# Last slot of a 16-batch transformer kernel: the last batch's gated result in two token halves, routing sums moved to ScalarE, and products that nobody reads in a pause of TensorE

## The reference, cut to what matters

```
# L1 attention, per head of 64 values
o = chunk_retention(rotary(q), rotary(k), v)
o = o * rsqrt(mean(o*o) + EPS) * gnorm_w
o = o * (g * sigmoid(g))
x = x + o @ Wo.T
# L1 feed-forward: half of the tokens of a batch are routed
h = layernorm(x); scores = h @ w_router
top_scores, top_idx = top_k(scores, 256)
update = sigmoid(top_scores) * (gelu(h[top] @ W1 + b1) @ W2 + b2)
x = x + 0.5 * (h with the update added at top_idx)
```

## Time and profile before

| | us |
|---|---|
| median of 3 runs | 805.19 |
| the profiled execution | 807.99 |
| its span, first to last instruction | 805.8 |
| TensorE busy | 757.8 (94%) |
| VectorE busy | 665.8 (83%) |
| ScalarE busy | 424.5 (53%) |
| GpSimd busy | 475.3 (59%) |
| mean granted clock of TensorE | 0.977 |

### The profile page before, as it was taken

The page is one execution under the profiler, slowest core; times in us unless marked ns, Lnnn a source line. Parts: engine busy times, 40 slices in busy tenths (PEclk is TensorE's granted clock), DMA queues, the critical chain, the costliest instruction groups (busy, mean ns, idle before and its releaser), DMA issues.

```text
span 805.8 us, 29577 instructions
## 1 busy us (share of the span) xinstructions
PE 757.8 (94%) x13001; PEld 614.8 (76%) x13001; DVE 665.8 (83%) x1825; ACT 424.5 (53%) x875; POOL 475.3 (59%) x375
## 2 busy tenths in 40 slices
PE   5778999999999999998999999999999999999875
PEld 4666888787887787776878888877888888878653
DVE  6686888888888999997858889987777988888887
ACT  2333555565555565654554446655544565564745
POOL 4467888887888888876543444444434344453544
PEclk9996999999999999999999999999999999999988
DMA  7000100011111110010000000000000000000113
GB/s 229 30 28 29 29 28 16 16 28 29 29 28 30 28 29 2 3 55 3 1 2 2 3 3 2 2 2 2 3 2 2 3 2 2 3 2 16 55 39 105
DMA packets 23284, 18.57 MB, mean 23 GB/s; under 512 B 2146, under 2 KB 20468, under 8 KB 22900
## 3 DMA queue, kind: packets, MB, share of 16 engines
q1 hardware_dynamic: 22596, 16.40, 7.0%
q10 hardware_dynamic: 560, 0.28, 0.1%
HBM read 12.48 MB, written 4.19 MB: 21 GB/s over the span
## 4 chain that ended last, share of the span: by engine, by line
PE 75%; DVE 17%; POOL 3%; ACT 2%; issue 1%; DMA 0%; DVEq 0%; POOLq 0%; ACTq 0%
PE ps L286 20%; PE ps L410 11%; PE ps L401 10%; PE ps L281 5%; PE ps L675 4%; PE ps L364 3%; PE ps L308 3%; PE ps L297 3%; PE ps L384 3%; PE ps L394 2%; POOL grstd L1067 2%; PE ps L356 2%; DVE x L1225 2%; PE ps L667 2%; PE ps L320 2%; PE ps L685 2%
## 5 line engine op out<-in xcount | busy, mean ns | idle before, releaser
L1067 POOL TENSOR_TENSOR grstd<-gve,mhalf 128x32 f32<-128x32 f32 (+1 forms) x32 | 159.0, 4968 | 26.5 <-DVE gve L1280 26.5
L410 PEld LDWEIGHTS ps<-w_s,hid 128*128 128x128 f32 x1024 | 123.5, 192 | 9.0 <-issue 8.0
L410 PE MATMUL ps<-w_s,hid 128*128 128x128 f32 x1024 | 129.0, 277 | 0.7 <-issue 0.7
L401 PE MATMUL ps<-xt_r,w_s 128*128 128x512 f32 x256 | 126.7, 617 | 0.7 <-ACT xt_r L822 0.7
L826 ACT ACTIVATE hid<-ps,b_s 128x512 f32<-128x512 f32 x128 | 84.0, 726 | 24.0 <-PE ps L401 23.8
L1063 POOL TENSOR_TENSOR r_ret<-ve_ret,powers 128x8 f32<-128x8 f32 x32 | 57.8, 1807 | 27.6 <-DVE ve_ret L1211 27.6
L286 PE MATMUL ps<-w_qkvg,xt_p 128*128 128x128 f32 x512 | 71.2, 285 | 2.8 <-ACT xt_p L822 2.8
L1073 POOL TENSOR_TENSOR um<-um 128x96 f32<-128x96 f32 (+1 forms) x32 | 21.3, 665 | 88.5 <-DVE um L1259 88.5
L401 PEld LDWEIGHTS ps<-xt_r,w_s 128*128 128x128 f32 x256 | 45.2, 192 | 35.1 <-issue 30.1
L1058 POOL TENSOR_TENSOR rstd_ln_mod<-ve_ln_mod,mhalf 128x4 f32<-128x4 f32 x32 | 32.3, 1010 | 65.3 <-DVE ve_ln_mod L1211 65.3
L1253 DVE TENSOR_TENSOR sc<-ps,tri 128x1024 f32<-128x1024 f32 (+1 forms) x64 | 58.3, 953 | 15.1 <-PE ps L320 7.6
(11 more groups left out here) (236 smaller groups left out, 1749.8 us busy)
## 6 DMA issues: line engine op xcount, KB each, us to landing
xtin<-in_xt SPq DMA_DIRECT2D x16, 256.0 KB, 3.8
out_x<-base SPq DMA_DIRECT2D x16, 256.0 KB, 2.3
xin<-in_x SPq DMA_DIRECT2D x15, 256.0 KB, 3.0
rot<-in_rot SPq DMA_DIRECT2D x2, 1024.0 KB, 5.9
w_s<-in_w SPq DMA_DIRECT2D x2, 256.0 KB
xin<-in_x ACTq DMA_DIRECT2D x1, 256.0 KB, 4.0
w_qkvg<-in_wqkvg SPq DMA_DIRECT2D x1, 256.0 KB, 3.8
w_qkv<-in_wqkv SPq DMA_DIRECT2D x1, 256.0 KB
```

Source lines behind the costliest of these rows:

```text
L401: nc.tensor.matmul(bank(k), w1_s[:, f, :], xt["r"][:].rearrange("p j n -> p (j n)"), start=True, stop=True).then_inc(s[f"h{f}"], 1)
L410: mm = nc.tensor.matmul(bank(k, j * P, P), hid[:, f, j * P:(j + 1) * P], w2_s[:, f, :], start=False, stop=(f == last and j == NT - 1), ski ...
L1067: nc.gpsimd.tensor_tensor(grstd[:, 0:n], gve[:, 0:n], mhalf[:, 0:n], ALU.pow) \
```

## The change

In the last slot:

1. Batch 15's y is transposed with a signal after each half (two token tiles). Squares, sums over heads, the powers and the final multiplication go by halves. y is multiplied by the gate first (signal yg), by the norm's factor second (gy_half). The transposes of the gated result, their copies and the output products go by halves as well.
2. TensorE issues 18 products of the identity with itself into bank 6 behind the transposes of y (keep_busy(18, X1)), and 5 such products in the first slot. Nobody reads them.
3. The base of batches 14 and 15 is computed by ScalarE, four instructions each (scaled_base), from x2 with a scale 1 + 0.5 rstd and a bias of half the negative mean; VectorE makes these two small columns (base_weights) instead of keep_base. Batch 15 uses the buffer x2b.
4. The order on TensorE and VectorE changes: routed_up(1) goes behind the output products; scaled_sum and variance of batch 15 go from behind rank_try(5) to behind rank_try(3), the negative mean of batch 15 from behind rank_above to behind rank_try(4); last_sum(0) goes ahead of routed_up(1) of batch 15.

```diff
+            def keep_busy(times, k):
+                for _ in range(times):
+                    nc.tensor.matmul(bank(k, 0, P), ident, ident, start=True, stop=True)
...
                 if g < 0:
+                    keep_busy(5, 2)
...
# TensorE, slot_end
-                transpose_y(now)
+                wait(pe, "ycopy", now)
+                for half in range(2):
+                    for c in (2 * half, 2 * half + 1):
+                        for k in range(2):
+                            at = YB * BANK + c * VF + k * P
+                            mm = nc.tensor.transpose(PS[:, at:at + P], qm[:, k, c * P:(c + 1) * P], ident)
+                    mm.then_inc(s["y_half"], 1)
+                keep_busy(18, X1)
                 wait(pe, "ln_mod_xn", old)
                 wait(pe, "ystore", sl.count(-2))
                 transpose4("ln_mod", h, X2)
-                rank_sum(3, 2, 1)
+                gated_half(0)
                 wait(pe, "ln_mod_xt", old)
                 routed_up(0, X1)
+                rank_sum(3, 2, 1)
+                gated_half(1)
+                output_half(0)
+                output_half(1)
+                rank_sum(3, 3, 1)
                 routed_up(1, 3)
-                transpose_gated(now, YB)
-                rank_sum(3, 3, 1)
                 wait(pe, "act0", old)
                 routed_up(2, X1)
-                output_b(now, (0, 1))
                 rank_sum(3, 4, 1)
-                output_b(now, (2, 3))
                 wait(pe, "act1", old)
                 routed_up(3, 3)
                 rank_sum(3, 5, 1)
...
                 routed_up(0, X1)
+                last_sum(0, 1)
                 wait(pe, "act3", old)
                 routed_up(1, 3)
-                last_sum(0, 1)
...
# ScalarE
+            def copy_half(half):
+                wait(act, "tg_half", half + 1)
+                nc.scalar.copy(gt[:, :, 2 * half * P:2 * (half + 1) * P].rearrange("p k (j n) -> p j k n", j=2),
+                               bank(YB + half).rearrange("p (j k n) -> p j k n", j=2, k=2)).then_inc(s["gt_half"], 1)
+
+            def scaled_base(b, src, n, count):
+                wait(act, "base_w", n + 1)
+                for j in range(NT):
+                    last = nc.scalar.activation(base[:, b * S + j * P:b * S + (j + 1) * P], src[:, j, :], ACT.Identity,
+                                                bias=base_w[:, n, 1, j:j + 1], scale=base_w[:, n, 0, j:j + 1])
+                last.then_inc(s["base"], 1)
...
                 route_weight(3)
+                copy_half(0)
                 hidden(0, X1, old)
+                copy_half(1)
+                scaled_base(sl.batch(-1), x2, 0, old)
                 hidden(1, 3, old)
-                copy_gated(now, YB)
                 hidden(2, X1, old)
                 weigh(7)
                 hidden(3, 3, old)
-                normalise(now)
+                normalise(now, x2b)
                 copy_xt("ln_mod", xt["r"], X2, now)
                 store_y(2, sl.batch(-1), old)
+                scaled_base(sl.batch(0), x2b, 1, now)
...
# GpSimd
                 root("ln_mod", old)
-                group_root(4 * H1, now)
-                wait(pool, "gy", now)
+                for half in range(2):
+                    at = slice(2 * half * H1, 2 * (half + 1) * H1)
+                    wait(pool, "gve_half", half + 1)
+                    nc.gpsimd.tensor_tensor(grstd[:, at], gve[:, at], mhalf[:, at], ALU.pow).then_inc(s["grstd_half"], 1)
+                wait(pool, "gy_half", 2)
                 for n in range(3, 6):
                     add_output(n)
                 root("ln_mod", now)
...
# VectorE
-                head_sums(H1, V1, sl)
-                negative_mean(old)
+                half_sums(0, sl)
+                half_sums(1, sl)
+                base_weights(0, old)
+                for half in range(2):
+                    at = slice(half * S, (half + 1) * S)
+                    wait(dve, "sq_half", half + 1)
+                    nc.vector.tensor_tensor(t2[:, at], bank(YB + half), gate[sl.buf(0)][:, at], ALU.mult) \
+                        .then_inc(s["yg"], 1)
+                normed_half(0)
                 rank_narrow(3, 1, 1)
                 rank_try(2)
-                keep_base(sl.batch(-1), old)
-                head_norm(H1, V1, now)
-                wait(dve, "yn", now)
-                nc.vector.tensor_tensor(t2[:], t2[:], gate[sl.buf(0)][:], ALU.mult).then_inc(s["gy"], 1)
+                normed_half(1)
                 rank_narrow(3, 2, 1)
                 rank_try(3)
+                scaled_sum(BT["wo"], r_ret[sl.buf(0, 4)][:, 0, :], x1[sl.buf(0, 4)], x2b, "wo", "x2", now)
+                variance("ln_mod", x2b, ve["ln_mod"], now)
                 rank_narrow(3, 3, 1)
                 rank_try(4)
+                base_weights(1, now)
                 rank_narrow(3, 4, 1)
                 rank_try(5)
-                wait(dve, "base", old)
-                scaled_sum(BT["wo"], r_ret[sl.buf(0, 4)][:, 0, :], x1[sl.buf(0, 4)], x2, "wo", "x2", now)
-                variance("ln_mod", x2, ve["ln_mod"], now)
                 rank_narrow(3, 5, 1)
                 rank_above()
-                negative_mean(now)
                 rank_between()
                 rank_order()
                 rank_choose()
-                keep_base(sl.batch(0), now)
                 last_load(YB)
```

More of the change, by code:

```diff
@@ L743, in slot_b, with gated_half, output_half @@
                 states_b((0, 1), True, BT["state"], sl)
+            def gated_half(half):
+                wait(pe, "gy_half", half + 1)
+                for j in range(2):
+                    for k in range(2):
+                        at = (2 * half + j) * VF + k * P
+                        mm = nc.tensor.transpose(bank(YB + half, (2 * j + k) * P, P), t2[:, at:at + P], ident)
+                mm.then_inc(s["tg_half"], 1)
+            def output_half(half):
+                wait(pe, "gt_half", half + 1)
+                for j in (2 * half, 2 * half + 1):
+                    for k in range(2):
+                        mm = nc.tensor.matmul(bank(BT["wo"], j * P, P), gt[:, k, j * P:(j + 1) * P], w_o1[:, k, :],
+                                              start=(k == 0), stop=(k == 1), skip_group_check=True)
+                if half == 1:
+                    mm.then_inc(s["wo"], 1)
             def slot_end(sl):
```

41 lines of the change are left out of this document (35 added, 6 removed).

## The result

The changed kernel took 810.51 us (median of 4 runs, 809.0 to 812.49) against 805.76 us for the kernel before (4 runs, the three that were known and one more, 804.76 to 808.63): ratio 1.0064, interval 1.0032 to 1.0095. In a second comparison, over 12 runs, it took 808.92 us, ratio 1.0039, interval 1.0018 to 1.006. It is slower. A ratio, with its 95% interval, is that of the whole comparison and not the quotient of the two medians; the two differ by up to 0.11% here.

What follows compares the result with a forecast made beforehand. It took the last slot to be bound by when last_load can start, behind VectorE's search and TensorE's last_rows. Terms +2.3, -0.3 and +1.8 gave +3.8 on 805.19, so 809.0 us; 8-in-10 range 803.2 to 810.8.

Steps and rivals of the forecast that it cites:

- The two causes that it named: Last slot: the search's sixth round comes late (+2.3 us), and TensorE's clock falls once more (+1.8 us); chance 0.43.
- The order of the others changes nothing: Last search's sums on TensorE: only last_sum(0) ahead of routed_up(1) matters, ending a 0.28 us VectorE wait; -0.3 us.
- The clock's term: TensorE's queue after the thin stretch from 775.1 to 781.2 us begins at half clock: +1.8 us, bounds 0 and 3.4.
- The late search: Last slot: k_rank of round 5 comes 3.3 us later, so TensorE's queue ends last_rows(15) 2.3 us later.
- The products: The 18 products behind y's transposes take 4.2 us, hidden in TensorE's pause, and should keep the clock up: nothing.
- The rival that they don't hold the clock: Behind y's transposes, h's transposes and routed_up stay at half clock: about 810.9 us; 0.14 shared with an earlier fall.
- The clock falls around the gated halves too: Rival: after 767.2 us TensorE's transposes and output products run at half clock, +1.5 us, 810.5 us; 0.14 shared.
- The powers: GpSimd's 8-column powers for batch 15's halves take 1.81 us each, ready before VectorE wants them; at 2.90, 1.7 later.
- last_sum(0): Last search: the sum goes ahead of routed_up(1) of batch 15, so VectorE's 0.28 us wait goes; -0.3 us.
- The first slots: The 5 products are hidden and gain 0; a rival has them keep the clock, mostly about 803.5 us, chance 0.18.
- One of its own signs of being wrong: First slot: a clock of 1.0 at 22 us, where half clock was expected as before, would show the forecast wrong.
- The rival that VectorE's wait isn't there: Before batch 15's negative mean: weigh(7) and add_output come in time, the 1.9 us wait goes, 805.3 us; chance 0.09.

Runs made afterwards that it cites:

- e10_thin: Changed kernel with 9 unread products added on TensorE ahead of rank_sum(4) and 9 ahead of rank_sum(5): 807.57 us, ratio 1.0012 to the kernel before.
- e9_sum0: Changed kernel with TensorE's work moved ahead of rank_sum(4) and rank_sum(5), GpSimd's root ahead of add_output(5), last_sum(0) back behind routed_up(1): 804.85 us, ratio 0.9989.
- e2_root: Changed kernel with GpSimd's root for batch 15's layer norm moved ahead of add_output(5): 808.27 us, ratio 1.0033 to the kernel before.
- e4_no5: Changed kernel without the 5 unread products in the first slot: 809.95 us, ratio 1.005 to the kernel before.
- e5_b18: Kernel before with only the 18 unread products added behind the transposes of y: 804.08 us, ratio 0.9977.
- e12_b18: Kernel before with only the 18 unread products added behind y's transposes, timed a second time: 804.71 us, ratio 0.9978.

## Where the prediction held, and the steps that failed

It said 809.0 us on 805.19, ratio 1.0047, with 807.9 to 810.1 as the forecast's own range. The measured 810.51 us lies above that range, though inside the wide one, to 810.8; the second comparison, 1.0039, would be 808.3 us and lies inside both. The two causes that it named are both shown, and the slot got longer by more than their sum. Two of its steps failed:

- "The order of the others changes nothing, as their sums come while VectorE does its own steps." The term was -0.3 us. It came out at -0.25 for the wait and +0.52 for the last four combines, +0.3 together.
- The clock's term, 1.8 us (1.5 to 2.4), was too small: 2.1, 2.4 and 2.9 us in the three profiled executions with this last slot.

From y's transposes to the end of the span these three executions take 4.4, 4.7 and 5.2 us more than the kernel before, where the prediction had 3.8. On top of it comes a pause ahead of y's transposes that it had no term for: +1.5, +0.9 and 0 us. The two aren't independent: the later the pause lets the work come, the less of it meets the fall of the clock.

The prediction's times were from the start of the span; measured from y's transposes (762.01 before, 760.74 after) they compare like this:

| step, us from y's transposes | predicted | measured |
|---|---|---|
| 18 products end | 5.2 | 5.1 |
| output of batch 15 | 11.3 | 11.2 |
| scaled_sum and variance end | 14.1 | 14.1 |
| weigh(7) ends | 15.1 | 14.9 |
| GpSimd's root ends | 17.4 | 17.2 |
| VectorE's wait for it | 1.9 | 1.95 |
| k_rank of round 5 | 19.2 | 19.0 |
| last_rows(15) ends at full clock (e10_thin) | 26.8 | 26.4 |
| the clock's part | 1.8 | 2.1 |
| last_rows(15) ends | 28.6 | 28.5 |

- **The late search** (+2.3): 1.95 in e10_thin, net of the 1.25 us that the 18 products give back. The two chains I added up, VectorE's order and the path weigh(7), add_output(5), root, held to 0.2 us.
- **The clock** (+1.8): 2.1 to 2.9. The fall came where it was forecast (16.7 us behind y's transposes, forecast 16 to 19). Its price was taken from 3.0 to 4.8 us of work at half clock, as in the one fall of the kernel before; here it was 4.5 to 6.2 us of a fall of 6.8. e10_thin, which fills the pauses and changes nothing else there, measures it. That the work meets more or less of the same fall from one execution to the next is the part that one trace couldn't show.
- **The products** at nothing: right, as their 4.18 us lay in the pause, at granted clock 1.00 (the stage from 761.67). The rival that they don't hold the clock is out.
- **The clock falls around the gated halves too**: out, granted 1.00 from 767.00 to 771.90, with 4.63 of 4.90 us busy. This stretch mixes transposes with products, and so tells nothing for or against the rule that was weighed there (the Trainium skill, "TensorE: Matmul & The Clock Gate", Part 4).
- **The powers** at 1.81 us each: 1.62 (3.24 for two). Hidden either way. The bound of 2.90 us for 16 columns was the reading of one instruction; the sixteen of this shape in the kernel before take 3.76 us on average.
- **last_sum(0)** (-0.3): the first failed step. It did gain 0.25, but moving routed_up(1) behind the sum delayed hidden(1), weigh(8) and so all of GpSimd's add_outputs; its weighted output then ran beside VectorE's last combines. This is VectorE's row for the four of them (duration in ns: least, median, greatest):

```profile
L1347 DVE SCALAR_TENSOR_TENSOR base<-yall,wcol,base x4: 339/572/1417, 802.4 to 804.7; 128x128 f32<-128x128 f32 x4
```

Before, one of the four was long (1.35 us, beside GpSimd's L1176), and the sum was 2.15 us; now the first takes 0.80 us beside L1223 and the second 1.42 beside L1226, and the sum is 2.67. e9_sum0 undoes this in its trace; in the times, 0.9989 for 0.998, it can't be told, and the two ran on different chips. The Trainium skill, "SBUF — State Buffer", section "SBUF: two separate sides", says that a VectorE operation with two SBUF inputs and a GpSimd operation that reads SBUF take a shared pair of ports in turn, the loser blocked for the whole instruction; the trace agrees, 0.34 becoming 1.4 beside a GpSimd operation of 1.26 us, and 0.16 becoming 1.02 in e2_root.
- **The pause of 1.2 us before L396**: no term had it. TensorE stops after 51 of 64 instructions of one loop (61 in three of the kernels), waiting for nothing that the profile shows. It is 0 in 4 of the 14 profiled executions and 0.53 to 1.17 in the others. Some expectations above call it a pause in instruction supply; what the traces show of this is the following. The output stores don't separate the two kinds: they begin 5.8 us behind the slot's start in all 14. The 16 KB transfer on the DMA queue that the profile names "instruction" does: the last one ahead of the loop's end (at 6.3 us) stands 2.65 to 3.05 us behind the slot's start in the four executions without the pause, and at 4.40 to 5.05 in the ten with it, the latest beside the longest pause. That TensorE waits for this transfer is likely by that, and not shown; no run moves it.
- **The first slots** at nothing: not told from nothing on the mean (e4_no5). One of its own signs of being wrong did appear, the clock at 1.0 at 22 us, and the profiled pair alone would have told the other story, 2.7 us of gain with the clock at 0.91 for 0.87.
- **The rival that VectorE's wait isn't there** (805.3) took 1.9 us for the wait and left the clock's fall out. e2_root, which removes the wait, gains 1.07 us at round 5, and the clock still falls.

The measured ratios, 1.0064 and 1.0039, are 5.2 and 3.1 us on 806, and the sum of 3.8 stands between them. That is luck in part and no proof of each term: the combines, part of the clock and the pause were missing from it, the first slots came out 2.7 us earlier in the profiled pair, and single runs spread by more than that. The terms are shown by the table above and by e10_thin, not by the agreement of the totals.

## What to carry to other kernels

A value that one engine's strict queue waits for must be followed beyond its first reader: here the output of batch 15 came 4.2 us earlier (11.2 us behind y and not 15.4), and the kernel got slower, since a search round had been put behind it and half of TensorE's queue behind that round. Before moving work onto another engine, add up the busy time of the engine that sets the pace over that stretch: here it falls by 0.65 of 20.23 us, so there was little to win, and 18 unread products on the old order were as good as the whole change repaired. When an instruction of another engine is moved to end a wait, look at what then runs beside the instruction that waited: here a wait of 1.95 us became one instruction of 1.02. Compare a stage from its own start: the stages ahead of it move by more, from execution to execution, than most edits are worth. And take the price of a fall of the clock from more than one execution.

## What the hardware showed that I hadn't expected

- TensorE's pause inside a loop of 64 independent instructions, with the clock at 1.00 on both sides and no semaphore in it: 0 to 1.17 us, and longest where the transfer on the instruction queue came latest (5.05 us behind the slot's start).
- A 128x4 VectorE instruction of 0.16 us took 1.02 us beside a GpSimd addition of 1.26 us, in all five kernels where the two met.
- The clock in the first 80 us isn't a property of the kernel alone: mean 0.87, 0.91, 0.93 or 0.96, and one kernel shows two of these (e5_b18, e12_b18).
- Once the pauses before it held unread products, TensorE kept its full clock with only 0.45 us of idle time in front of each rank_sum (e10_thin); without them it fell to half behind a wait of 2.42 us and 1.1 us of product, and stayed there over a second wait of 2.46 us.
- A 128x8 power takes GpSimd 1.62 us, between 1.02 (128x4) and 2.90 (128x16); the sixteen powers of 128x16 take 3.76 on average, and 128x8 with other exponents takes 1.81.
